# Twenty-four transposes a batch moved from TensorE to DMA and VectorE in a two-layer attention kernel

## Time and profile before

| what | value |
|---|---|
| time, median of 3 runs | 3465.83 us (3462.2 to 3466.53) |
| the profiled execution's own time | 3466.39 us |
| its span, first to last instruction | 3464.6 us |
| granted TensorE clock, mean | 0.996 |
| TensorE busy (matmul / weight load) | 98% / 80% |
| VectorE, ScalarE, GpSimd busy | 61%, 53%, 31% |
| DMA | 332.1 MB, queue of SP 33.3% of 16 engines |

### The profile page before, as it was taken

One profiled execution on the slowest core, in us unless ns is written; L12 is line 12 of the kernel. 1 busy time (PEld: TensorE's weight loads), 2 busy tenths in 40 slices (PEclk: granted clock), 3 DMA queues, 4 the chain that ended last, 5 costly groups with the idle time before them and its releaser, 6 DMA issues.

```text
span 3464.6 us, 51840 instructions
## 1 busy us (share of the span) xinstructions
PE 3400.3 (98%) x16816; PEld 2776.6 (80%) x16816; DVE 2114.8 (61%) x3452; ACT 1835.3 (53%) x3082; POOL 1064.7 (31%) x947
## 2 busy tenths in 40 slices
PE   8999999999999999999999999999999999999999
PEld 4788878888788887887778877788777888788887
DVE  4577456773577735786457854578455784557744
ACT  3577226772278622785227842378323882247822
POOL 0244213442034410354104531145211452114511
PEclk9999999999999999999999999999999999999999
DMA  8512235212443125341153312442224422343212
GB/s 314 159 40 62 92 111 146 55 57 84 132 120 90 33 92 145 88 98 72 45 171 80 80 74 66 149 98 62 92 58 137 98 62 92 83 140 70 61 55 73
DMA packets 109849, 332.10 MB, mean 96 GB/s; under 512 B 21744, under 2 KB 54768, under 8 KB 98800
## 3 DMA queue, kind: packets, MB, share of 16 engines
q1 hardware_dynamic: 109552, 328.45, 33.3%
HBM read 162.68 MB, written 31.49 MB: 56 GB/s over the span
## 4 chain that ended last, share of the span: by engine, by line
PE 87%; DVE 4%; DMA 3%; ACT 2%; issue 2%; SPq 1%; POOL 0%; ACTq 0%; DVEq 0%; POOLq 0%
PE big L468 24%; PE big L595 13%; PE ops L581 13%; PE tps L568 13%; PE ops L734 10%; PE big L665 7%; PE big L633 5%; PE ops L468 3%; DMA ST<-ST 1%; SPq L384 1%; DMA d_m<-PT 1%; ACT PB L849 1%; DVE X L1369 1%; DMA d_u<-ST 1%; ACT PB L938 0%
## 5 line engine op out<-in xcount | busy, mean ns | idle before, releaser
L989 POOL TENSOR_SCALAR PB<-PB,small 128x1024 f32<-128x1024 f32 x576 | 651.8, 1132 | 1325.4 <-DVE small L1219 1314.6
L1213 DVE TENSOR_REDUCE small<-big 128x1 f32<-128x1024 f32 x512 | 625.0, 1221 | 100.9 <-PE big L595 97.6
L1224 DVE TENSOR_TENSOR PT<-tps,PT 128x512 fp32r<-128x512 f32 x1024 | 651.8, 678 | 32.4 <-ACT PT L855 32.0
L855 ACT ACTIVATE PT<-tps 128x512 fp32r<-128x512 f32 x1024 | 566.3, 597 | 147.6 <-PE tps L568 144.9
L849 ACT ACTIVATE PB<-big,small 128x1024 f32<-128x1024 f32 x512 | 572.1, 1117 | 100.6 <-DVE small L1213 97.6
L581 PE MATMUL ops<-PT,VT 128*128 128x512 f32 x2048 | 599.1, 414 | 0.0
L595 PE MATMUL big<-ST 128*128 128x512 f32 x2048 | 555.0, 393 | 10.2 <-DMA ST<-ST 10.2
L568 PEld LDWEIGHTS tps<-ident,PB 128*128 128x128 f32 x4096 | 467.4, 140 | 116.2 <-DVE PT L1224 55.9
L568 PE MATMUL tps<-ident,PB 128*128 128x128 f32 x4096 | 551.4, 275 | 8.9 <-DVE PT L1224 6.1
L595 PEld LDWEIGHTS big<-ST 128*128 128x128 f32 x2048 | 383.1, 188 | 98.4 <-issue 12.6
L581 PEld LDWEIGHTS ops<-PT,VT 128*128 128x128 f32 x2048 | 346.1, 189 | 47.2 <-DVE PT L1224 5.0
(11 more groups left out here) (151 smaller groups left out, 4803.9 us busy)
## 6 DMA issues: line engine op xcount, KB each, us to landing
ST<-ST SPq DMA_DIRECT2D x384, 256.0 KB, 5.0
W<-d_qk SPq DMA_DIRECT2D x32, 1024.0 KB, 6.3
W<-PB SPq DMA_DIRECT2D x256, 128.0 KB, 2.4
XA<-in_x SPq DMA_DIRECT2D x8, 2048.0 KB, 7.6
X<-in_x SPq DMA_DIRECT2D x8, 2048.0 KB, 10.6
W<-d_wp SPq DMA_DIRECT2D x8, 2048.0 KB, 11.9
W<-d_g SPq DMA_DIRECT2D x8, 2048.0 KB, 12.3
W<-d_m SPq DMA_DIRECT2D x8, 2048.0 KB, 7.8
```

What stands on the lines that cost most here:

```text
L855: act_fn(pt_slot(u, s)[:, 0, :], tps[n % 2][:], ACT.Copy).then_inc(s_pt_hi, 1)
L989: nc.gpsimd.tensor_scalar(PB[:, i, :], PB[:, i, :], rinv[:, i:i + 1], 1.0, ALU.mult, ALU.mult)\
L1213: V.tensor_reduce(negmax[:, i:i + 1], tile(("s", 4 * u + tb))[:], axis=AX.X, op=ALU.max, negate=True).then_inc(s_row_max, 1)
L1224: V.tensor_tensor(pt_slot(u, s)[:, 1, :], tps[n % 2][:], pt_slot(u, s)[:, 0, :].bitcast(f32), ALU.subtract).then_inc(s_pt_ready, 1)
```

## The change

Six units a batch, u = 0, 1, 4, 5, 8 and 9 (the first two of each of the first three pairs), are `MOVED`. Of their eight slots, s = 0 to 3 stay with TensorE; s = 4 to 7 (`MOVED_SLOTS`, 24 a batch of 128) take another way:

- `exps` of a moved unit writes its tile in another order of keys: inside each half of 512 keys, the key s*128 + k goes to column 4*k + s. ScalarE's writes are then 16 bytes apart, and the transposes that remain read their 128 columns 16 bytes apart.
- SP's `move_quarters(u)` waits for the unit's four normalised tiles (and from the second unit on for the squares of the moved unit before), and issues 16 transfers, each of 32 partitions by 4 tiles by 128 columns (64 KB, runs of 512 bytes), from the second half of `PB` into `F0`, which is X[:, 0:2].
- VectorE's `square` turns 32x32 blocks, one instruction of 128x512 for a slot, from `F0` (read 16 bytes apart) into X[:, 2:4]. It stands at the end of a step, for the slots n+2 and n+3: slots 4 and 5 at the end of step 4u+6, slots 6 and 7 at the end of step 4u+7. The first of a unit waits for all 16 transfers.
- `pt_hi` and `pt_lo` read these slots from X and not from `tps`; `pt_hi` waits for the square, and for `values0` of the slot four earlier (`s_slot_free`), as no transpose orders it any longer.
- X now serves as a buffer until unit 9 has been turned. So its load moves from the batch's beginning to behind `stack_head(3, 0)` and a wait for slot 7 of unit 9 (`s_pt_ready` 80), ahead of the load of `d_g`; `scale_x` moves to tiles 50, 52, 54 and 56.

```diff
+def moved_units(pairs):
+
+    return [u for pair in range(pairs) for u in (4 * pair, 4 * pair + 1)]
+
+MOVED = moved_units(PAIRS - 1)
+MOVED_SLOTS = [8 * u + s for u in MOVED for s in range(4, NT)]
-X_SCALE_STEPS = (20, 23, 26, 29)
+X_SCALE_STEPS = (50, 52, 54, 56)
...
+        F0 = X[:, 0:2, :].rearrange("p a (b n) -> p (a b) n", n=HALF).rearrange("p q (t n) -> p q t n", t=KB)
+        def squared(s):
+            return X[:, 2 + (s - 4) // 2, HALF * (s % 2):HALF * (s % 2) + HALF]
...
+                def move_quarters(u):
+                    half = u % 2
+                    sp.wait_ge(s_p_norm, b * 72 + 4 * u + 4)
+                    own_wait(sp)
+                    if u:
+                        sp.wait_ge(s_squared, squared_count(b, 8 * MOVED[MOVED.index(u) - 1] + NT - 1))
+                    own_wait(sp)
+                    for tq in range(QUARTERS):
+                        for sq in range(QUARTERS):
+                            sp.dma_start(F0[32 * sq:32 * sq + 32, tq, :, :],
+                                         PB[32 * tq:32 * tq + 32, 4 * half:4 * half + 4,
+                                            HALF + P * sq:HALF + P * sq + P]).then_inc(s_moved[half], 16)
...
-                sp.dma_start(X[:], src_x(b)).then_inc(s_x_res, 16)
                 sp.wait_ge(s_v_full, b * 4 + 4)
                 own_wait(sp)
+                move_quarters(0)
                 for i in (2, 3):
                     sp.dma_start(w_qk(i)...
+                move_quarters(1)
                 stack_head(b, 1, 0)
                 sp.dma_start(W[1][:].bitcast(f32), d_wp[:]).then_inc(s_ld_wp, 16)
                 stack_head(b, 1, 1)
+                move_quarters(4)
+                move_quarters(5)
                 stack_head(b, 2, 0)
                 stack_head(b, 2, 1)
+                move_quarters(8)
+                move_quarters(9)
                 stack_head(b, 3, 0)
+                sp.wait_ge(s_pt_ready, b * 144 + 80)
+                own_wait(sp)
+                sp.dma_start(X[:], src_x(b)).then_inc(s_x_res, 16)
                 sp.dma_start(W[0][:].bitcast(f32), d_g[:]).then_inc(s_ld_g, 16)
                 stack_head(b, 3, 1)
...
                     for t in range(4):
-                        last = nc.tensor.transpose(tps[n % 2][:, P * t:P * t + P],
-                                                   PB[:, 4 * (u % 2) + t, P * s:P * s + P], ident[:])
+                        row = PB[:, 4 * (u % 2) + t, :]
+                        if u in MOVED:
+                            keys = row[:, 0:HALF].rearrange("p (k s) -> p s k", s=4)[:, s, :]
+                        else:
+                            keys = row[:, P * s:P * s + P]
+                        last = nc.tensor.transpose(tps[n % 2][:, P * t:P * t + P], keys, ident[:])
...
-                        transposes(n // 8, n % 8)
-                        transposes(n // 8, n % 8 + 1)
+                        for m in (n, n + 1):
+                            if m not in MOVED_SLOTS:
+                                transposes(m // 8, m % 8)
...
+                    to, scores = PB[:, i, :], t[:]
+                    if u in MOVED:
+                        to = to.rearrange("p (h q r s) -> p h s q r", h=2, q=QUARTERS, s=4)
+                        scores = scores.rearrange("p (h s q r) -> p h s q r", h=2, q=QUARTERS, s=4)
+                    act_fn(to, scores, ACT.Exp, bias=negmax[:, i:i + 1], accum_out=rowsum[:, i:i + 1])\
...
+                    if n in MOVED_SLOTS:
+                        act.wait_ge(s_squared, squared_count(b, n))
+                        act.wait_ge(s_slot_free, squared_count(b, n))
+                        turned0 = squared(s)
...
+                def square(n):
+                    u, s = n // 8, n % 8
+                    if s == 4:
+                        dve.wait_ge(s_moved[u % 2], moved_count(b, u))
+                    V.transpose(squared(s).rearrange("p (t q r) -> p t q r", t=KB, q=QUARTERS),
+                                F0.rearrange("p q t (r s) -> p s t q r", s=4)[:, s - 4, :, :, :])\
+                     .then_inc(s_squared, 1)
...
                         pt_lo(n // 8, n % 8 + 1)
+                    for m in (n + 2, n + 3):
+                        if m in MOVED_SLOTS:
+                            square(m)
```

More of the change, by code:

```diff
@@ L163, in turned, with t_count, squared_count, moved_count @@
             return PB[:, 4 * c + s // 2, HALF * (s % 2):HALF * (s % 2) + HALF]
+        F0 = X[:, 0:2, :].rearrange("p a (b n) -> p (a b) n", n=HALF).rearrange("p q (t n) -> p q t n", t=KB)
+        def squared(s):
+            return X[:, 2 + (s - 4) // 2, HALF * (s % 2):HALF * (s % 2) + HALF]
+        def t_count(b, n):
+            return b * (8 * UNITS0 - len(MOVED_SLOTS)) + len([m for m in range(n + 1) if m not in MOVED_SLOTS])
+        def squared_count(b, n):
+            return b * len(MOVED_SLOTS) + MOVED_SLOTS.index(n) + 1
+        def moved_count(b, u):
+            i = MOVED.index(u)
+            return (b * (len(MOVED) // 2) + i // 2 + 1) * EXCHANGE
         def by_quarter(row):
@@ L228, in build @@
         s_pt_ready = sem("pt_ready")
+        s_moved = [sem("moved_even"), sem("moved_odd")]
+        s_squared = sem("squared")
+        s_slot_free = sem("slot_free")
         s_o_full = sem("o_full")
@@ L584, in values0 @@
                         last.then_inc(s_o_full, 1)
+                    elif n + 4 in MOVED_SLOTS:
+                        last.then_inc(s_slot_free, 1)
                 def scores0(u, tb):
@@ L848, in exps @@
                     i = 4 * (u % 2) + tb
-                    act_fn(PB[:, i, :], t[:], ACT.Exp, bias=negmax[:, i:i + 1], accum_out=rowsum[:, i:i + 1])\
+                    to, scores = PB[:, i, :], t[:]
[3 more added lines that the diff above has]
+                    act_fn(to, scores, ACT.Exp, bias=negmax[:, i:i + 1], accum_out=rowsum[:, i:i + 1])\
                         .then_inc(s_exp_done, 1)
@@ L853, in pt_hi @@
                     n = 8 * u + s
-                    act.wait_ge(s_t_full, b * 128 + n + 1)
-                    act_fn(pt_slot(u, s)[:, 0, :], tps[n % 2][:], ACT.Copy).then_inc(s_pt_hi, 1)
+                    if n in MOVED_SLOTS:
+                        act.wait_ge(s_squared, squared_count(b, n))
+                        act.wait_ge(s_slot_free, squared_count(b, n))
+                        turned0 = squared(s)
+                    else:
+                        act.wait_ge(s_t_full, t_count(b, n))
+                        turned0 = tps[n % 2][:]
+                    act_fn(pt_slot(u, s)[:, 0, :], turned0, ACT.Copy).then_inc(s_pt_hi, 1)
                 def corr(u, part):
@@ L1223, in pt_lo @@
                     dve.wait_ge(s_pt_hi, b * 144 + n + 1)
-                    V.tensor_tensor(pt_slot(u, s)[:, 1, :], tps[n % 2][:], pt_slot(u, s)[:, 0, :].bitcast(f32),
+                    turned0 = squared(s) if n in MOVED_SLOTS else tps[n % 2][:]
+                    V.tensor_tensor(pt_slot(u, s)[:, 1, :], turned0, pt_slot(u, s)[:, 0, :].bitcast(f32),
                                     ALU.subtract).then_inc(s_pt_ready, 1)
+                def square(n):
[5 more added lines that the diff above has]
+                     .then_inc(s_squared, 1)
                 for j in range(4):
```

## The result

| | median of runs | lowest to highest | profiled run | granted clock |
|---|---|---|---|---|
| before (4 runs, with the three of the section on the time before among them) | 3466.18 us | 3462.20 to 3467.74 | 3466.4 | 0.996 |
| after (4 runs) | 3778.28 us | 3771.02 to 3781.68 | 3771.02 (span 3769.2) | 0.965 |

The ratio is 1.0900 (95% interval 1.0881 to 1.0918): the change costs 312 us. The sign was forecast, the size was not: 3591 us was the forecast, and 3778 lies above the whole range to 3690. It lies where rival C does, 3630 to 3800.

What follows compares the result with a forecast made beforehand. TensorE, busy for 98% of the span, was taken to bound the kernel, with VectorE almost abreast. The profiled 3466.4 us plus 125 for late data and VectorE's order gave 3591 us, range 3470 to 3690.

Steps and rivals of the forecast that it cites:

- rival C: Exps, squares and weight loads with strided accesses cost double: A plus up to 210 us, 3630 to 3800; chance 14%.
- VectorE's order, data in time: Even with data in time, an odd unit loses 0.9 us, an even one wins 0.4: 12 us in 24 pairs.
- late data: At VectorE's squares, transfers land after the q/k part is due: units late by 2.2, 1.3 or 3.1 us.
- accesses 16 bytes apart: Weight loads, squares and exps reading or writing one float of every 16 bytes: taken as none, together up to 210 us.
- what is removed: TensorE's transposes of 24 slots a batch, 0.395 us each: 76 us in 8 batches, the most that can be won.
- T: Start of the score tile of projection step 7 in the second shown batch, 977.63 us; later times count from it.
- Layer 1's moves: Existing transfers taken as the model: sixteen took 10.34 us to issue, 0.65 apart, with 2.4 us from issue to landing.
- Rival B: Transfers land in good time and VectorE's order decides: 3478 us, range 3462 to 3500; chance 13%.
- A: The forecast itself, data late at VectorE's squares: 3591 us, own range 3555 to 3630; chance 62%.
- X's later load: X's load, now ahead of d_g and stack_head(3, 1), before head 1's scores: taken as 0, bound 3 us a batch.
- `scale_x` in steps 50 to 57: GpSimd time beside four a_lo: taken as 0, bound 0.5 us each, 2 a batch.

Runs made afterwards that it cites:

- plain kernel without transfers: The changed kernel with exp writes, weight loads and squares' reads contiguous, and the 16 transfers and the wait for them left out: 3528.3 us, ratio 1.0181.
- all plain: The changed kernel with exp writes, weight loads and squares' reads contiguous, every transfer, instruction and wait kept: 3634.6 us, ratio 1.0486.

## Why the prediction was wrong in size

The 312 us come apart by differences of medians:

| step | forecast | measured |
|---|---|---|
| VectorE's order, data in time | +12 | 3475.8 - 3466.4 = +9 |
| subtraction with both operands in SBUF | not seen | 3528.3 - 3475.8 = +53 |
| late data | +113 | 3634.6 - 3528.3 = +106 |
| accesses 16 bytes apart | 0, bound 210 | 3778.3 - 3634.6 = +144 |

**Right: what is removed and why little of it is won.** In the plain kernel without transfers the products of slots 4 and 5 of an even unit wait for `pt_lo`, as forecast, and not for the transposes (scores of step 4u+7, the products, scores of step 4u+10):

```profile
991.87 1.07 PE L645 MATMUL big<-ST 128*128 128x512 f32 x4
...
995.38 1.33 PE L629 MATMUL ops<-PT,VT 128*128 128x512 f32 x4 [0.59 <-DVE PT L1283]
...
1002.44 1.08 PE L645 MATMUL big<-ST 128*128 128x512 f32 x4
```

The scores of step 4u+10 start 10.57 us after those of 4u+7, in the kernel before 10.98 (988.61 - 977.63): 0.41 won, and 0.4 was forecast. The agreement is in part luck. The products began at T+3.51, when the first of the two subtractions was done, and not at T+4.1, and the projection behind them was 0.85 us ahead of before (T+4.68 for T+5.53); 0.44 of that was lost again by step 4u+10.

**Right: the data come late, by the issue of sixteen transfers.** Layer 1's moves were the right rows: 0.60 us an issue in both, whatever the bytes, and 189 us of waits. Rival B falls with it, and so does what it rested on: by an estimate from the 138 GB/s that the Trainium skill, SBUF — State Buffer, section The DMA setup-cost knee, gives for transfers of 64 KiB, 1 MiB would have been over in 7.6 us. Here SP's issues alone took 11.50, halving the bytes left the time as it was (3631.5 for 3634.6), and halving the number took the whole 106 us away. The size came out right (106 for 113) in part by luck. The 113 were all waiting; by the pages of the kernels with and without transfers, TensorE's time without work grew by 67 us (227.6 for 160.3) and its busy time, at the same work, by 40 (3405.7 for 3365.3).

**No term held the clock.** Its share can be estimated from TensorE's busy time in kernels with the same instructions: 3339.0 us with the operand in PSUM, 3365.3 without transfers, 3405.7 all plain, 3478.2 the changed kernel, at granted clocks of 0.998, 0.991, 0.979 and 0.965. By this some 26 of the 53, 40 of the 106 and 73 of the 144 us are products that ran longer (in the last the longer loads are included), and the rest is waiting.

**Wrong, the largest: "I take none, since no row shows such a price".** This term of the sum was 0 and measured 144 us, nearly half of the 312. Absence of a row was read as absence of a cost, for three kinds of instruction: the exps of 24 tiles a batch, the squares of 24 slots and the weight loads of the 24 slots that stayed. Measured: exp +1.00 us (2.12 for 1.12), square +0.40 (1088 for 688 ns), load +0.07. By the bounds these were 1.1, 0.6 and 0.1, so each lay close under its end. The rule that was cited for rival C, the Trainium skill, Advanced Engine Details and Errata, section Memory Cachelines (two hits on a line of 16 bytes for full pace), agrees with them: one hit a line cost 1.9 times on ScalarE's writes and 1.6 on VectorE's reads. With 14% it was given the weight of a mishap, where every access of the change met its condition. How the three reach the end of the program differs from their prices: exp 55, squares 86, loads at most 9. The exp has room on ScalarE but for the even units of the second and third pair, the square stands on VectorE between the landing and the q/k part, and the load runs beside the matmuls.

**Wrong, unforeseen: 53 us.** The line of the change that reads X in place of `tps` was costed at nothing, as an edit of an address. Both operands of the subtraction then lie in SBUF, and beside a GpSimd instruction it waits: two took 2.49 to 2.51 us for 1.27. An odd unit ended 1.2 us later by this (10.33 for 9.11), in 24 units 29 us; most of the rest is TensorE's longer busy time (26 us, above), as the clock falls from 0.998 to 0.991. The Trainium skill, SBUF — State Buffer, section Who interferes with whom, states that a VectorE instruction with two inputs in SBUF contends with a GpSimd instruction that reads SBUF, and that the shared port is an exclusive lock. The traces agree on both sides: 944 for 680 ns on VectorE, 1197 for 1132 on GpSimd, and both gone when the operand was back in PSUM. The rows of before had a hint as well, in layer 1's own subtraction (groups of the kernel before):

```profile
L1392 DVE TENSOR_TENSOR ST<-PB,ST 128x512 fp32r<-128x512 f32 x32 | 27.2, 867 | 0.0
L1392 DVE TENSOR_TENSOR W<-PB,W 128x512 fp32r<-128x512 f32 x32 | 21.0, 674 | 1.6 <-ACT W L948 1.4
```

One shape, one engine, both operands in SBUF, and 867 against 674 ns. The timeline shows what differs: two of these subtractions take 2.21 us while GpSimd normalises two tiles, and one takes 0.65 while GpSimd rests (VectorE, GpSimd, VectorE):

```profile
1308.85 2.21 DVE L1392 TENSOR_TENSOR ST<-PB,ST 128x512 fp32r<-128x512 f32 x2
...
1307.16 2.77 POOL L989 TENSOR_SCALAR PB<-PB,small 128x1024 f32<-128x1024 f32 x2
...
1332.56 0.65 DVE L1392 TENSOR_TENSOR ST<-PB,ST 128x512 fp32r<-128x512 f32 x1
```

**The range.** Its upper end, 3690, took "the lower third of C" on top of A. C's own range, 3630 to 3800, held the result, but not by C's mechanism alone: strides cost 144 of its up to 210 us, and the unforeseen 53 fell into the room that the bound left.

**Not tested alone:** X's later load and `scale_x` in steps 50 to 57, taken as 0. They are in the kernel that ends 9.4 us over the kernel before. An odd unit's 0.86 lost (9.11 for 8.25) less an even unit's 0.41 won is 11 us in 24 pairs, so by this estimate nothing is left for them.

## What to carry to other kernels

An edit that only changes where or in what order an instruction reads or writes can have a price even if no row shows one: ask of each operand whether consecutive elements share 16 bytes, and whether both inputs of a VectorE instruction lie in SBUF while GpSimd works. For many small transfers count the issues on a queue, not the bytes, and split them over two queues before anything else: in the version with even units only, that turned +2.5% into -0.7%. And where a wait as long as these (4.4 us) is put ahead of TensorE, add the products right behind it at about half the pace.

## What the runs showed of the hardware

- One fp32 of every 16 bytes: ScalarE's 128x1024 write 2.12 us for 1.12; VectorE's 32x32 transposes 1088 ns for 688; TensorE's weight load 67 ns more, of which 6 ns reach the time.
- An issue of 32 partitions by 4 runs took 0.60 us on SP at 32, 64 and 128 KB alike, and 0.56 us on GpSimd.
- A subtraction of 128x512 with both operands in SBUF: 944 ns in the mean for 680, up to twice as long for a pair beside GpSimd (2.51 us for 1.27), and GpSimd's normalising of 128x1024 1197 ns in the mean for 1132.
- After 4.37 us without work TensorE's granted clock was 0.54 over the next 3.5 us, and four score products took 2.07 us for 1.07.
